# The last step of a triangular solve: the guess added by VectorE at the eviction, not by an identity product on TensorE

## The chip, the cores and the metric

The kernel runs on one core of a Trainium2 chip, as one program. Its engines are TensorE (PE in the profile, with its weight loads as PEld), VectorE (DVE), ScalarE (ACT), GpSimd (POOL) and SyncE (SP), which issues nearly all of the transfers. Each engine works through its own list of instructions in order and waits on semaphores. The metric is the device time of one execution in microseconds; less is better. Times of a run are compared with runs of the kernel before.

## The reference

The input is 4 sequences of 256 tokens with 256 features. A layer norm, then a gated delta rule with 16 key heads and 32 value heads of 128, then a layer norm and a mixture of experts. What matters here is the inner part, cut to this:

```python
T = solve_triangular(eye + M, eye, lower=True)      # M: strictly lower, from k k^T, decay, beta
v_c = einsum('bhnij,bhnjd->bhnid', T, v_beta)
k_cumdecay = einsum('bhnij,bhnjd->bhnid', T, k_beta * exp(g)[..., None])
def step(state, inp):
    attn = einsum('bhcd,bhed->bhce', q_i, k_i) * dec_i
    v_new = v_i - einsum('bhcd,bhde->bhce', kcd_i, state)
    out_i = einsum(q_i * exp(g_i), state) + einsum(attn, v_new)
    state = state * exp(g_last) + einsum(k_i * exp(g_last - g_i), v_new)
```

So for each chunk a triangular system is solved for `v_new`, and the output is made from it.

## The kernel before

The 256 tokens of a sequence are two chunks of 128 (c = 0 and 1). A **group** is one key head with its two value heads; there are 16 groups. In a group each of the 4 sequences b is a unit, and two units (b = 0, 1 or b = 2, 3) are a **pair**, handled by one set of instructions: 2 sequences times 2 value heads, 512 columns.

For a pair the inverse of the unit triangular matrix is built in f16 by seven rounds of doubling (steps `x`, `w` on PE; `xe` on ScalarE; `t`, `u` on VectorE). `u16` then holds the transposed inverse. The inverse is only good to f16, so each right-hand side is solved with one step of correction, per chunk c:

- `y0` (PE, L690): guess = inverse times right side, into the PSUM bank `Y_BANK`.
- `g` (ScalarE, L1029): copies it to the f16 tile `y0`.
- `y1` (PE, L702 and L705): applies the system to the guess in `R_BANK` (one identity product, eight products with `n16` and `nl16`), and at the end, L708, puts the guess itself into `Y_BANK` by a product with the identity.
- `rr` (VectorE, L1318): residual = values less `R_BANK`, f16.
- `y2` (PE, L714): adds inverse times residual to `Y_BANK`.
- `vn` (ScalarE, L1035): copies `Y_BANK` to the tile `vn`, which is `v_new`.

For c = 0 there follow `v0s` (GpSimd, L1617, `vn` times a decay), `p` (PE, L724, the state's part of the second right side) and `r1h` (VectorE, L1325), with which c = 1 begins. `o` (PE, L741 and L744) makes the output of a unit from `vn`, `v0s`, `at` and `qx`; `sqr`, `ln`, `rex` (ScalarE), `hsum` (GpSimd), `ss` (PE), `hz` and `ht` (VectorE) normalize and gate it; `hth` (ScalarE) and `htl` (GpSimd, L1565) split it in two f16 halves, and `proj` (PE, L767) projects it.

Beside this runs the input side of a later group: `fill` and `rest` (PE, L582) project a half kind of 512 tokens into one of two banks, `evict` (ScalarE, L919) takes it out with the last tap of a causal convolution of four taps, and three `tap` steps (VectorE, L1229) add the others from the same bank. There are 24 taps a group. The bank is free for the fill after the next when the third tap is done: fill number r waits until 3(r-2)+3 taps are done. Taps 2, 5, 8 and so on to 20 and 23 are thus the ones that PE waits for. `kk` (PE, L636 and L621), `mask` (VectorE, L1265), `cross` (ScalarE, L998) and `nt` (VectorE, L1274) prepare the triangular matrices of a unit.

The order is written out by hand: `TABLE` is one list of steps with their number, unit and lag in groups. `sequence()` walks the list 24 times, and each engine takes from it the steps that it has a function for, in that order. A step's place on its engine is therefore its place in the table, whichever engine that is. One walk is called a period below. The four `vn` steps of a walk are

```python
("tap", 0, None, 0), ("vn", 1, 2, 2), ("tap", 1, None, 0)
("t", 0, 2, 1), ("vn", 0, 0, 1), ("tap", 20, None, 0)
("y2", 1, 0, 1), ("eye", 1, 0, 0), ("t", 5, 2, 1), ... ("vn", 1, 0, 1)
("y2", 0, 2, 1), ("mask", 0, 0, 0), ("fill", 16, None, 0), ("vn", 0, 2, 1)
```

(chunk, first unit of the pair, lag). They are called C (1, 2, 2), A (0, 0, 1), B (1, 0, 1) and D (0, 2, 1) in the text. A step with lag L handles group n - L in walk n, so B, D and A occur in walks 1 to 16, C in walks 2 to 17, and the taps in walks 0 to 15.

Of the kernel before, what the change touches and what calls it, by code (L numbers as in the profile page):

```python
# [10 lines left out]
ALU = mybir.AluOpType  # L11
# [147 lines left out]
def build(nc, x, wqkvz, wba, convw, dtb, alog, normw, wout, wm, b1, b2, rw, rb, c32, eye16, lev, gsc, rowsc, out):  # L159
    ctx = ExitStack()  # L160
    with ctx:
# [75 lines left out]
        hz = sb("hz", [P, 2, 512])  # L237
# [165 lines left out]
        def turn(U):  # L403
            return unit_index(U) // 2 % 2
# [125 lines left out]
        def _(pe):  # L530
# [163 lines left out]
            def y1_(U, c):  # L694

                G, b = U
                wait_p(pe, s_y0, U, 2, c + 1)
                wait_u(pe, s_nl, (G, b + 1), 1, 1)
                if c == 0:
                    wait_p(pe, s_r, (G, b - 2), 2, 2)  # L700
                guess = y0[:].rearrange("p b v d -> p (b v d)")
                nc.tensor.matmul(R_BANK[:, :], eye[:, 0], guess, start=(c == 0), stop=False, skip_group_check=True)  # L702
                for n, (two, v) in enumerate(FOUR):
                    for part in (n16, nl16):
                        mm = nc.tensor.matmul(R_BANK[:, n * P:(n + 1) * P], part[:, turn(U), 4 * two + 2 * v + c], y0[:, two, v],  # L705
                                              start=False, stop=(part is nl16), skip_group_check=True)
                mm.then_inc(s_a, 1)
                nc.tensor.matmul(Y_BANK[:, :], eye[:, 0], guess, start=True, stop=False, skip_group_check=True)  # L708

            def y2_(U, c):  # L710

                wait_p(pe, s_r, U, 2, c + 1)
                for n, (two, v) in enumerate(FOUR):
                    mm = nc.tensor.matmul(Y_BANK[:, n * P:(n + 1) * P], u16[:, turn(U), 4 * two + 2 * v + c], rr[:, two, v],  # L714
                                          start=False, stop=True, skip_group_check=True)
                mm.then_inc(s_y, 1)

            def p(U, _):
# [137 lines left out]
        def _(act):  # L856
# [171 lines left out]
                    wait_p(act, s_a, U, 2, 1)  # L1028
                nc.scalar.copy(y0[:].rearrange("p b v d -> p (b v d)"), Y_BANK[:, :]).then_inc(s_y0, 1)  # L1029

            def solved(U, c):
                G, b = U
                wait_p(act, s_y, U, 4, 2 * c + 2)
                wait_u(act, s_o, (G, b - 3), 1, 1)
                nc.scalar.copy(vn[:, turn(U), :, :, c].rearrange("p b v d -> p (b v) d"),  # L1035
                               Y_BANK[:, :].rearrange("p (n d) -> p n d", n=4)).then_inc(s_vn, 1)

            def squares(U, _):
                G, b = U
                wait_u(act, s_o, U, 1, 1)  # L1040
# [58 lines left out]
            def end(F, i):  # L1099
                end_of(0, i)  # L1100

            attention({"gate": gate, "evict": evict, "hi": high_weights, "silu": silu, "nexp": norm, "cap": cap, "exb": row_factors,
                       "exp": factors, "cross": cross_, "n16": high_n, "xe": xe, "g": guess, "vn": solved,
                       "sqr": squares, "ln": log_mean, "rex": inverse_root, "hth": high_output, "end": end})

            def high(n):
# [20 lines left out]
        def _(dve):  # L1127
# [183 lines left out]
            def residual(U, c):  # L1311
# [4 lines left out]
                else:  # L1316
                    wait_p(dve, s_y, U, 4, 2)
                nc.vector.tensor_tensor(rr[:], values(U, c), R_BANK[:, :].rearrange("p (b v d) -> p b v d", b=2, v=2),  # L1318
                                        ALU.subtract).then_inc(s_r, 1)

            def right_side(U, _):
                G, b = U
                wait_p(dve, s_p, U, 1, 1)
                wait_p(dve, s_y, (G, b - 2), 4, 4)
                nc.vector.tensor_tensor(r1h[:], values(U, 1), R_BANK[:, :].rearrange("p (b v d) -> p b v d", b=2, v=2),  # L1325
                                        ALU.subtract).then_inc(s_r1h, 1)
# [153 lines left out]
            def end(F, i):  # L1480
                end_of(0, i)

            attention({"gate": gate, "tap": tap, "lo": low_weights, "sc": scalars, "nmul": norm, "mask": mask, "nt": decayed, "t": t,
                       "u": u, "rr": residual, "r1h": right_side, "hz": hz_, "ht": ht_,
                       "acc": acc_, "end": end})


# [239 lines left out]
```

## Time and profile before

| | |
|---|---|
| median of 3 runs | 1333.41 us (1332.9 to 1334.39) |
| the profiled execution: time, span | 1335.4 us, 1333.6 us |
| mean granted TensorE clock | 0.985 of full speed |
| busy share PE, PEld, DVE, ACT, POOL | 91%, 65%, 78%, 68%, 57% |
| chain that ended last, by engine | PE 73%, DVE 12%, issue 8%, ACT 3%, POOL 2% |
| one period in the middle of the run | 60.4 us |

The busy share is the time in which an engine had an instruction running. PE's is high for a reason beside work: matmuls overlap, and a row's duration holds time in which the next one already runs. Two starts in a row say more than one duration. The same holds for DVE and ACT, whose next instruction starts before the one ahead has ended. In the chain, "issue" is time in which an engine waited for nothing that the profile shows.

### The profile page before, as it was taken

The numbers are of one execution on the slowest core, as the hardware profiler recorded it, in microseconds if no ns is written. First come the engines' busy times: TensorE is split into PE (matmuls) and PEld (weight loads), VectorE is DVE, ScalarE is ACT, GpSimd is POOL, SyncE is SP. The second block draws the span as 40 slices with busy tenths as digits, with TensorE's granted clock in tenths as the row PEclk, the third lists the DMA queues.
The fourth block names the chain that finished last, engine by engine and source line by source line (L and its number), as shares of the span: only waits on it lengthen the run. The fifth ranks groups of instructions, "written<-read, shape, count | busy, mean of one in ns | idle before, by whom it ended". The sixth has DMA issues, their size and how long they took to land.

```text
span 1333.6 us, 32082 instructions
## 1 busy us (share of the span) xinstructions
PE 1217.2 (91%) x11612; PEld 863.4 (65%) x11612; DVE 1037.8 (78%) x1641; ACT 903.4 (68%) x1715; POOL 756.3 (57%) x792
## 2 busy tenths in 40 slices
PE   3678999999999999999999999999977589999997
PEld 2346676767767676767667676767665356666664
DVE  5586979888797979888897979798865676666565
ACT  2668888888978888888878888888863222222221
POOL 1255666667666766667665766666676667444100
PEclk9999999999999999999999999999999789999999
DMA  3111110101111111101110111100110056445331
GB/s 112 36 57 34 33 38 29 42 25 41 33 58 31 35 34 33 41 26 42 33 57 13 54 33 33 42 26 17 32 35 25 24 168 201 142 146 157 111 103 40
DMA packets 51623, 75.64 MB, mean 57 GB/s; under 512 B 8358, under 2 KB 27208, under 8 KB 51468
## 3 DMA queue, kind: packets, MB, share of 16 engines
q1 hardware_dynamic: 51396, 73.46, 18.0%
q8 instruction: 94, 1.54, 0.5%
q14 instruction: 61, 0.50, 0.1%
q10 hardware_dynamic: 72, 0.14, 0.0%
HBM read 72.26 MB, written 1.32 MB: 55 GB/s over the span
## 4 chain that ended last, share of the span: by engine, by line
PE 73%; DVE 12%; issue 8%; ACT 3%; POOL 2%; DMA 1%; SPq 1%; DVEq 0%; ACTq 0%; POOLq 0%
PE bank L582 15%; PE products L537 9%; PE bank L830 9%; DVE sil L1229 7%; PE products L767 6%; PE products L753 4%; PE products L741 4%; PE products L636 3%; PE bank L665 3%; PE bank L673 3%; PE bank L645 3%; PE bank L601 2%; PE bank L724 2%; PE products L621 2%; PE bank L705 2%
## 5 line engine op out<-in xcount | busy, mean ns | idle before, releaser
L582 PE MATMUL bank<-xT,whl 128*128 128x512 f16 x1152 | 296.6, 384 | 26.8 <-DVE sil L1229 26.7
L1229 DVE SCALAR_TENSOR_TENSOR sil<-bank,cw,sil 128x510 f32<-128x510 f32 (+2 forms) x384 | 283.4, 738 | 16.1 <-ACT sil L919 12.1
L582 PEld LDWEIGHTS bank<-xT,whl 128*128 128x128 f16 x1152 | 98.7, 98 | 125.3 <-DVE sil L1229 38.8
L1110 ACT ACTIVATE kq<-vtok 128x512 f16<-128x512 f32 x94 | 59.1, 630 | 177.1 <-DVE vtok L1499 176.0
L1288 DVE CAST_PREDICATED t<-levm,bank 128x512 f16<-128x512 uint8 x192 | 136.2, 710 | 39.0 <-PE bank L665 36.3
L1499 DVE SCALAR_TENSOR_TENSOR vtok<-products,b1s,zs 128x512 f32<-128x512 f32 x94 | 70.5, 750 | 87.4 <-PE products L537 87.1
L1300 DVE CAST_PREDICATED u<-levm,bank 128x512 f16<-128x512 uint8 x192 | 135.4, 705 | 0.0
L1017 ACT ACTIVATE x<-bank 128x512 f16<-128x512 f32 x160 | 96.2, 601 | 54.1 <-PE bank L645 52.7
L1565 POOL TENSOR_TENSOR hthl<-hz,hthl 128x512 f16<-128x512 f32 x64 | 74.2, 1159 | 93.8 <-ACT hthl L1054 93.8
L1624 POOL TENSOR_TENSOR at<-kqm,ex 128x256 f32<-128x256 f32 x128 | 102.7, 807 | 26.1 <-issue 14.5
L767 PE MATMUL products<-wohl,hthl 128*128 128x256 f16 x768 | 96.8, 277 | 9.3 <-POOL hthl L1565 8.9
L1588 POOL TENSOR_TENSOR hsq<-hsq,qsq 128x512 f32<-128x512 f32 x64 | 81.9, 1280 | 38.2 <-ACT hsq L1042 38.1
L919 ACT ACTIVATE sil<-bank,cw 128x512 f32<-128x512 f32 x128 | 87.7, 685 | 16.7 <-PE bank L582 15.8
L645 PEld LDWEIGHTS bank<-t,n 128*128 128x128 f16 x1536 | 67.6, 98 | 44.7 <-DVE t L1288 27.7
L1631 POOL TENSOR_TENSOR qx<-cross,exb 128x256 f32<-128x256 f32 x128 | 94.0, 734 | 2.3 <-ACT exb L985 2.3
L741 PE MATMUL products<-at,vn 128*128 128x128 f32 x512 | 82.4, 283 | 8.8 <-ACT cross L998 6.2
L977 ACT ACTIVATE ex<-grow,sc 128x128 f32<-128x128 f32 x256 | 86.3, 396 | 0.1
L645 PE MATMUL bank<-t,n 128*128 128x64 f16 x1536 | 77.3, 193 | 8.2 <-DVE t L1288 8.2
L767 PEld LDWEIGHTS products<-wohl,hthl 128*128 128x128 f16 x768 | 72.4, 99 | 19.0 <-issue 10.7
L1505 DVE SCALAR_TENSOR_TENSOR kq<-vtok,kq 128x512 f16<-128x512 f32 x94 | 80.3, 854 | 2.2 <-ACT kq L1110 2.1
L665 PEld LDWEIGHTS bank<-x,u 128*128 128x128 f16 x1280 | 53.5, 97 | 44.0 <-ACT x L1017 40.3
L741 PEld LDWEIGHTS products<-at,vn 128*128 128x128 f32 x512 | 67.1, 191 | 19.6 <-issue 11.3
(219 smaller groups left out, 3086.2 us busy)
## 6 DMA issues: line engine op xcount, KB each, us to landing
grow<-rowsc SPq DMA_DIRECT2D x64, 256.0 KB, 3.3
wt<-wqkvz SPq DMA_DIRECT2D x16, 768.0 KB, 4.4
wt<-wm SPq DMA_DIRECT2D x47, 256.0 KB, 2.8
zs<-gsc SPq DMA_DIRECT2D x35, 256.0 KB, 3.4
wo<-wout SPq DMA_DIRECT2D x16, 256.0 KB, 3.2
zs<-gsc SPq DMA_DIRECT2D x16, 224.0 KB, 3.1
zs<-gsc SPq DMA_DIRECT2D x16, 192.0 KB, 3.1
zs<-gsc SPq DMA_DIRECT2D x17, 160.0 KB, 3.3
```

The costliest lines, as they stand in the source:

```text
L537: mm = nc.tensor.matmul(dst, stationary(h, k), moving(l, k), start=(n == 0), stop=(n == len(terms) - 1))
L582: mm = nc.tensor.matmul(dst[:, :], whl[:, h, k, col:col + HD], xT[:, l, k, half * 512:(half + 1) * 512], start=(k == 0 and m == 0), stop=( ...
L645: mm = nc.tensor.matmul(X_BANK[:, m * 64:(m + 1) * 64], N[:, m], r, start=True, stop=True)
L741: mm = nc.tensor.matmul(dst, vn[:, turn(U), b % 2, v, c], at[:, nth(U), v, c], start=(v == 0 and c == 0), stop=(c == 0), skip_group_check= ...
L767: mm = nc.tensor.matmul(KB_BANK[:, c * D:(c + 1) * D], hthl[:, parity(U), h, v, c], wohl[:, q, l, v], start=(n == 0), stop=(n == len(terms ...
L830: mm = nc.tensor.matmul(bank[4 + t // 2][:, (t % 2) * D:(t % 2 + 1) * D], hid[:, n % HR, h, m * P:(m + 1) * P], lent[k % ring][:, l, D:2 * D],
L1017: ins = nc.scalar.mul(halves(X, n)[:, :, :, 0], packed(X_BANK, n), -1.0)
L1229: nc.vector.scalar_tensor_tensor(out=dst[:, :, late:S], in0=src[:, :, 0:S - late], scalar=cw[:, q, i, 3 - late:4 - late], in1=dst[:, :, la ...
L1288: nc.vector.copy_predicated(halves(t16[:, turn(U)], n)[:, :, :, 0], by4(2 * n, n), packed(X_BANK, n)).then_inc(s_tup, 1)
L1300: nc.vector.copy_predicated(halves(Ut, n)[:, :, :, 1], by4(2 * n + 1, n), packed(WT_BANK, n)).then_inc(s_uup, 1)
L1624: nc.gpsimd.tensor_tensor(at[:, nth(U), v], kqm[:, w, :, 1], ex[:, w, v], ALU.mult).then_inc(s_at, 1)
L1631: nc.gpsimd.tensor_tensor(qx[:, nth(U), v], cross[:, w], exb[:, w, v].unsqueeze(1).to_broadcast([P, 2, P]), ALU.mult).then_inc(s_qx, 1)
```

## The change

`y1` no longer puts the guess into `Y_BANK`; `y2` begins the sum in that bank itself; and `vn` moves from ScalarE to VectorE, where it adds the f16 tile `y0` to the bank as it evicts it. The table is not touched, so `vn` has the same place in it.

```diff
@@ in y1_ (PE)
                 mm.then_inc(s_a, 1)
-                nc.tensor.matmul(Y_BANK[:, :], eye[:, 0], guess, start=True, stop=False, skip_group_check=True)
@@ in y2_ (PE)
                     mm = nc.tensor.matmul(Y_BANK[:, n * P:(n + 1) * P], u16[:, turn(U), 4 * two + 2 * v + c], rr[:, two, v],
-                                          start=False, stop=True, skip_group_check=True)
+                                          start=True, stop=True)
@@ ScalarE
-            def solved(U, c):
-                G, b = U
-                wait_p(act, s_y, U, 4, 2 * c + 2)
-                wait_u(act, s_o, (G, b - 3), 1, 1)
-                nc.scalar.copy(vn[:, turn(U), :, :, c].rearrange("p b v d -> p (b v) d"),
-                               Y_BANK[:, :].rearrange("p (n d) -> p n d", n=4)).then_inc(s_vn, 1)
@@ VectorE
+            def solved(U, c):
+                G, b = U
+                wait_p(dve, s_y, U, 4, 2 * c + 2)
+                wait_u(dve, s_o, (G, b - 3), 1, 1)
+                nc.vector.tensor_tensor(vn[:, turn(U), :, :, c], Y_BANK[:, :].rearrange("p (b v d) -> p b v d", b=2, v=2), y0[:],
+                                        ALU.add).then_inc(s_vn, 1)
```

Each engine's list shows where the steps stand. The first place is VectorE at the end of the taps of a walk, around step A; `rr` is the residual of the same pair, `t` the first step of the next inverse, the `sil` rows are taps 18 to 21. Before:

```order
L1229 SCALAR_TENSOR_TENSOR sil<-bank,cw,sil 128x2x255
L1318 TENSOR_TENSOR rr<-vtok,bank 128x512
L1229 SCALAR_TENSOR_TENSOR sil<-bank,cw,sil 128x2x254
L1288 COPY_PREDICATED t<-levm,bank 128x512
L1229 SCALAR_TENSOR_TENSOR sil<-bank,cw,sil 128x2x253
L1300 COPY_PREDICATED u<-levm,bank 128x512
```

and of the change:

```order
L1221 SCALAR_TENSOR_TENSOR sil<-bank,cw,sil 128x2x255
L1310 TENSOR_TENSOR rr<-vtok,bank 128x512
L1221 SCALAR_TENSOR_TENSOR sil<-bank,cw,sil 128x2x254
L1280 COPY_PREDICATED t<-levm,bank 128x512
L1317 TENSOR_TENSOR vn<-bank,y 128x4x128
L1221 SCALAR_TENSOR_TENSOR sil<-bank,cw,sil 128x2x253
L1292 COPY_PREDICATED u<-levm,bank 128x512
```

The new `vn` stands ahead of tap 20, which frees a bank for PE.

The second place is VectorE at the beginning of the next group's taps, around step C. Before:

```order
L1274 TENSOR_TENSOR nt<-ex,kqm 128x512
L1229 SCALAR_TENSOR_TENSOR sil<-bank,cw,sil 128x2x255
L1229 SCALAR_TENSOR_TENSOR sil<-bank,cw,sil 128x2x254
L1288 COPY_PREDICATED t<-levm,bank 128x512
L1229 SCALAR_TENSOR_TENSOR sil<-bank,cw,sil 128x2x253
```

and of the change:

```order
L1266 TENSOR_TENSOR nt<-ex,kqm 128x512
L1221 SCALAR_TENSOR_TENSOR sil<-bank,cw,sil 128x2x255
L1317 TENSOR_TENSOR vn<-bank,y 128x4x128
L1221 SCALAR_TENSOR_TENSOR sil<-bank,cw,sil 128x2x254
L1280 COPY_PREDICATED t<-levm,bank 128x512
L1221 SCALAR_TENSOR_TENSOR sil<-bank,cw,sil 128x2x253
```

The `vn` of the pair before has come between tap 0 and tap 1, which work on the same rows of `sil`.

The third is VectorE around steps B and D; `u` 64x8x64 is the last round of an inverse, `kq` the normalized keys, `kqm` the step `mask`. Before:

```order
L1300 COPY_PREDICATED u<-levm,bank 128x16x32
L1303 CAST u<-bank 64x8x64
L1257 TENSOR_TENSOR kq<-sil,sq 128x4x256
L1348 SCALAR_TENSOR_TENSOR acc<-products,acc 128x512
L1318 TENSOR_TENSOR rr<-vtok,bank 128x512
L1265 TENSOR_TENSOR kqm<-products,cst 128x512
L1340 TENSOR_TENSOR hz<-hz,hsq 128x512
L1333 SCALAR_TENSOR_TENSOR hz<-products,zs 128x512
```

and of the change:

```order
L1292 COPY_PREDICATED u<-levm,bank 128x16x32
L1317 TENSOR_TENSOR vn<-bank,y 128x4x128
L1295 CAST u<-bank 64x8x64
L1249 TENSOR_TENSOR kq<-sil,sq 128x4x256
L1347 SCALAR_TENSOR_TENSOR acc<-products,acc 128x512
L1310 TENSOR_TENSOR rr<-vtok,bank 128x512
L1257 TENSOR_TENSOR kqm<-products,cst 128x512
L1317 TENSOR_TENSOR vn<-bank,y 128x4x128
L1339 TENSOR_TENSOR hz<-hz,hsq 128x512
L1332 SCALAR_TENSOR_TENSOR hz<-products,zs 128x512
```

B stands ahead of the last `u`, D between `mask` and `ht`.

## Rows read from the trace of the kernel before

**Rows 1.** The page: busy time of each engine over the span.

```profile
PE 1217.2 (91%) x11612; PEld 863.4 (65%) x11612; DVE 1037.8 (78%) x1641; ACT 903.4 (68%) x1715; POOL 756.3 (57%) x792
```

**Rows 2.** By stretch: us, busy us (count) PE, PEld, DVE, ACT, POOL; PEclk, DMA, GB/s.

```profile
402.49:462.87 60.38, 58.38 (x611) 42.43 (x611) 52.05 (x81) 51.66 (x100) 39.56 (x41) 1.00 0.12 37
402.50:411.00 8.50, 8.41 (x107) 5.40 (x108) 8.09 (x13) 7.71 (x18) 5.45 (x5) 1.00 0.01 2
433.40:462.87 29.47, 28.19 (x300) 19.51 (x299) 29.20 (x47) 24.37 (x48) 19.64 (x24) 1.00 0.14 40
```

**Rows 3.** Instructions of L708, L1035 and L1318: duration ns min/median/max, first and last start.

```profile
L708 PE MATMUL bank<-y,eye x64: 379/379/634, 96.3 to 1027.6; 128*128 128x512 f16 x64
...
L1035 ACT COPY vn<-bank x64: 573/585/588, 99.0 to 1028.9; 128x512 f32<-128x512 f32 x64
...
L1318 DVE TENSOR_TENSOR rr<-vtok,bank x64: 666/680/689, 97.8 to 1027.8; 128x512 f16<-128x512 f32 x64
```

**Rows 4.** Timeline around step A: start us, duration us, engine, line.

```profile
460.82 0.73 DVE L1229 SCALAR_TENSOR_TENSOR sil<-bank,cw,sil 128x508 f32<-128x508 f32 x1
460.98 0.38 PE L714 MATMUL bank<-rr,u 128*128 128x128 f16 x4
461.48 0.71 DVE L1288 CAST_PREDICATED t<-levm,bank 128x512 f16<-128x512 uint8 x1
462.09 0.72 DVE L1229 SCALAR_TENSOR_TENSOR sil<-bank,cw,sil 128x506 f32<-128x506 f32 x1
462.87 0.82 PE L582 MATMUL bank<-xT,whl 128*128 128x512 f16 x3 [0.21 <-DVE sil L1229]
```

**Rows 5.** Timeline around step C, VectorE and PE.

```profile
433.44 0.75 DVE L1229 SCALAR_TENSOR_TENSOR sil<-bank,cw,sil 128x510 f32<-128x510 f32 x1 [0.44 <-ACT sil L919]
434.31 0.75 DVE L1229 SCALAR_TENSOR_TENSOR sil<-bank,cw,sil 128x508 f32<-128x508 f32 x1
434.97 0.74 DVE L1288 CAST_PREDICATED t<-levm,bank 128x512 f16<-128x512 uint8 x1
435.59 0.74 DVE L1229 SCALAR_TENSOR_TENSOR sil<-bank,cw,sil 128x506 f32<-128x506 f32 x1
436.38 0.82 PE L582 MATMUL bank<-xT,whl 128*128 128x512 f16 x3
```

**Rows 6.** Timeline around step D.

```profile
422.50 0.69 DVE L1265 TENSOR_TENSOR kqm<-products,cst 128x512 f32<-128x512 f32 x1 [0.62 <-PE products L621]
423.11 0.68 DVE L1340 TENSOR_TENSOR hz<-hz,hsq 128x512 f32<-128x512 f32 x1
...
422.63 0.59 ACT L1035 COPY vn<-bank 128x512 f32<-128x512 f32 x1 [0.29 <-PE bank L714]
...
423.29 1.41 POOL L1617 TENSOR_TENSOR v0s<-vn,sc 128x512 f32<-128x512 f32 x1 [0.85 <-ACT vn L1035]
424.66 1.16 POOL L1565 TENSOR_TENSOR hthl<-hz,hthl 128x512 f16<-128x512 f32 x1
...
425.20 1.06 PE L724 MATMUL bank<-v0s,qx 128*128 128x128 f32 x8
426.09 1.47 PE L767 MATMUL products<-wohl,hthl 128*128 128x256 f16 x12
```

**Rows 7.** Timeline of PE: the removed product and what follows it, three places.

```profile
412.96 0.38 PE L708 MATMUL bank<-y,eye 128*128 128x512 f16 x1
413.18 0.40 PE L645 MATMUL bank<-t,n 128*128 128x64 f16 x8
...
420.69 0.38 PE L708 MATMUL bank<-y,eye 128*128 128x512 f16 x1
420.91 1.03 PE L636 MATMUL products<-kq 128*128 128x256 f32 x4
...
429.21 0.38 PE L708 MATMUL bank<-y,eye 128*128 128x512 f16 x1
429.58 1.10 PE L636 MATMUL products<-kq 128*128 128x256 f32 x4
```

More of the change, by code:

```diff
@@ L1102, in _ @@
             attention({"gate": gate, "evict": evict, "hi": high_weights, "silu": silu, "nexp": norm, "cap": cap, "exb": row_factors,
-                       "exp": factors, "cross": cross_, "n16": high_n, "xe": xe, "g": guess, "vn": solved,
+                       "exp": factors, "cross": cross_, "n16": high_n, "xe": xe, "g": guess,
                        "sqr": squares, "ln": log_mean, "rex": inverse_root, "hth": high_output, "end": end})
@@ L1483, in _ @@
             attention({"gate": gate, "tap": tap, "lo": low_weights, "sc": scalars, "nmul": norm, "mask": mask, "nt": decayed, "t": t,
-                       "u": u, "rr": residual, "r1h": right_side, "hz": hz_, "ht": ht_,
+                       "u": u, "rr": residual, "vn": solved, "r1h": right_side, "hz": hz_, "ht": ht_,
                        "acc": acc_, "end": end})
```

## The prediction

> **What bounds the kernel now.** I first read the busy times. PE is at 91% of the span, DVE at 78% [rows 1]. That alone would say that 64 matmuls less are a gain. PE's figure is inflated, though: a 512-column product is recorded with 379 ns [rows 3], yet the product after L708 starts 413.18 - 412.96 = 0.22 us after it, and 420.91 - 420.69 = 0.22 us at the second place [rows 7]. So one removed product is worth 0.22 us of PE at most, and all 64 of them 14.1 us.
>
> Next I asked for one period. The same fill starts at 402.49 and at 462.87, so a period lasts 60.38 us, in which DVE is busy 52.05 us [rows 2]: it has 8.3 us free, and four `vn` steps would want about 2.4. An average like this hides where the free time lies, so I cut the period. In the tap stretch, 433.40 to 462.87, DVE is busy 29.20 of 29.47 us [rows 2]: it has 0.27 us free in thirty. In the packed part, 402.50 to 411.00, PE is busy 8.41 of 8.50 us [rows 2]. The kernel thus has two regimes in each period: DVE paces the taps, PE what comes after. What the change is worth depends on which regime each of its pieces falls into.
>
> Then I read the places themselves, in the timeline. At the end of the taps PE starts a fill at 462.87, after 0.21 us idle put down to a tap; that tap started at 462.09 and lasted 0.72, so ended at 462.81 [rows 4]. At their beginning PE starts a fill at 436.38, and the tap that it needs ended at 435.59 + 0.74 = 436.33 [rows 5]. Both fills begin some 0.05 us after a tap's end: whatever delays those taps delays PE.
>
> **The price of the new step.** The trace has no sum of a PSUM bank and an f16 tile into an f32 tile. The nearest is `rr`, also a tensor-tensor operation of 512 columns with a PSUM bank and an SBUF tile, 680 ns [rows 3]. DVE starts the next instruction before the last has ended: 462.09 - 461.48 = 0.61 [rows 4], 435.59 - 434.97 = 0.62 [rows 5], 423.11 - 422.50 = 0.61 us [rows 6]. I take 0.60 as its turn on DVE and 0.68 until its result is there. Bounds: 0.60 if it overlaps as these do, 0.68 if its whole duration counts. On ScalarE the copy took 585 ns [rows 3].
>
> **The change part by part.**
>
> *Step A, ahead of tap 20.* The new `vn` goes between the `t` at 461.48 and the tap at 462.09. `y2` (L714) started at 460.98 with four products, 0.38 us in all, so its bank is complete at 461.36, 0.7 us before DVE comes to it [rows 4]: no wait, but the full 0.60 us, and the tap ends 0.60 us later. The fill moves from 462.87 to 463.47. After it PE is packed [rows 2] and cannot catch up. Behind `vn` on DVE wait tap 20, `u`, tap 21 and so on; all shift together. The walks with both step A and taps are 1 to 15: 15 x 0.60 = +9.0 us. PE's 0.22 us, saved here a little earlier, only makes it wait longer for the same tap: worth nothing.
>
> *Step C, between tap 0 and tap 1.* Tap 1 adds to what tap 0 has written, so it waits for its end: 433.44 + 0.75 = 434.19, started 434.31, while a tap's turn on DVE is only 434.97 - 434.31 = 0.66 us, so DVE was free at 434.10 [rows 5]. `vn` fits in part into this bubble: it starts at 434.10 and tap 1 at 434.70 in place of 434.31, that is +0.39 us. `t`, tap 2 and the fill at 436.38 shift with it. From there DVE has next to no free time until the end of the taps [rows 2], so the delay is still there at step A. Walks 2 to 15: 14 x 0.39 = +5.5 us. Bounds: 0.39 and 0.60 a walk (the bubble not used).
>
> *Step B* falls into the stretch where DVE waits for PE before the last round of `u`, and I cost it at nothing. The work that hides it is PE's way to that last round; without this cover it would cost its 0.60 us.
>
> *Step D.* DVE waits 0.62 us for PE [rows 6], does `mask` at 422.50, and now `vn` at 423.11 instead of ScalarE at 422.63 [rows 6]. Its result is there at 423.79, against 423.22 before: 0.57 us later. GpSimd waits for it: `v0s` started at 423.29, 0.07 after, and now starts at 423.86. With its 1.41 us it ends at 425.27, and `htl`, which started at 424.66, takes 1.16 us and now ends at 426.43. PE needs `htl` for `proj` at 426.09 [rows 6]: 0.35 us late (`p`, at 425.20, is late by 0.1 and hidden in it). `ht`, pushed to 423.71 by `vn`, ends at 424.39 and its halves are there before 425.27. If `v0s` takes less, D costs less: bounds 0 and 0.35. I take 0.35, since `v0s` lies beside the same DVE work as before. Walks 1 to 16: 16 x 0.35 = +5.6 us.
>
> *The product on PE.* The first two places, 412.96 and 420.69, lie after the packed part, with work right behind; I count 0.20 us each (bounds 0 and 0.22), since a copy on ScalarE and the keys' norm on DVE cap it a little. At the third, 429.21, the next product begins at 429.58, 0.37 us later and not 0.22 [rows 7]: it waits for something else, and the saving is lost. The fourth is at step A. Sum: 16 x 0.40 = -6.4 us.
>
> *The copy off ScalarE*: 64 x 0.585 us of an engine that is busy 68% [rows 1]. It stands on no path I could find, apart from making room at B, and I count nothing.
>
> Sum: 9.0 + 5.5 + 5.6 - 6.4 = +13.7 us. The profiled execution took 1335.4 us, so 1349.1; its time is 2.0 us above the median 1333.4, so I forecast **1347.1 us**, 1.0% slower.
>
> **A rule weighed against a row.** Two starts at 2.4 GHz (the granted clock is 1.00 in these stretches [rows 2]) lie 0.22 us apart for 512 columns [rows 7]. The Trainium skill, TensorE: Matmul & The Clock Gate, section Back-to-back issue gap, gives about 131 ns per matmul at N=512 in a sustained stream, and some 216 ns for an isolated one. By the first figure, as an estimate, the gain on PE would be 4.2 us and not 6.4, and the time 1349.3. The trace agrees with the second.
>
> **The rivals.**
>
> *PE is the bound and DVE has room.* The chain that ended last is 73% PE, and DVE has 8.3 us free in a period [rows 2]. If these took in all four `vn`, each product would give back its 0.22: 64 x 0.22 = -14.1 us, 1319.3. Against it stand the fills that start 0.05 us after a tap's end. It decides if taps 2 and 20 have at least 0.4 and 0.6 us of slack before their fills; a weaker form, in which only A, C and D are hidden and only two products count, gives -6.4 us, 1327.0. Chance together 0.08.
>
> *Little but A costs.* The shift at C is made up within the next 25 us, or D is absorbed: from 9.0 - 6.4 = +2.6 us to, with C kept in full, 9.0 + 5.5 - 6.4 = +8.1 us, 1336.0 to 1341.5. For it: DVE's 0.27 us free in the taps and `v0s` that may be shorter. Chance 0.20, of which 0.06 within 0.2% of before.
>
> *DVE is the bound throughout.* Every `vn` costs its turn and PE gives nothing back: 0.60 x (16 + 15 + 16 + 14) = +36.6 us, 1370.0. Against it: DVE waits 0.62 us for PE at D and 0.44 for ScalarE at C [rows 5, 6]. Some of it could still hold, if DVE comes to `vn` before `y2` is done and the taps stand behind it: at A there is 0.7 us to spare. A case of +20 us or more, 1353.4 and up, gets 0.10. DVE at 78% leads over PE's weight loads at 65% [rows 1]. The Trainium skill, Perfetto Trace Analysis, section Identifying the Most-Contended Engine, judges TensorE by its weight loads and would name DVE here, so it speaks against moving work there.
>
> **How the numbers follow.** The main case, DVE bound in the taps with step D late, has 0.62: its own bounds are 9.0 + 5.5 + 0 - 7.0 = +7.5 us, and with 0.68 a turn at A, 0.60 at C and one product of the two in vain, 10.2 + 8.4 + 5.6 - 3.2 = +21.0 us. The range for 8 in 10 leaves out the faster cases and the far end of the last rival: 1337 to 1354. A change of 0.2% (2.7 us) is about what a measurement of this kernel can tell from none. Faster 0.08, same 0.06, slower 0.86.
>
> **What the profile of the change should show.** A period of about 61.2 us in place of 60.38 (13.7 us over some 16 walks). L1317 on DVE 64 times with some 680 ns. At A the fill after tap 20 starts 0.6 us later against `t` of the same place, its wait grown from 0.21 to about 0.8. At C tap 1 starts 1.26 us after tap 0 in place of 0.87. At D `v0s` waits for DVE, and `proj` for `htl`. L708 gone, and at its third place the next product no earlier. The prediction is wrong if the fills behind taps 2 and 20 have come no later, if `vn` waits for `y2` on DVE, or if the shorter queue on ScalarE has brought evictions, and with them taps, forward.

## The result, and the profile after

| | before | after |
|---|---|---|
| median of 4 runs | 1333.9 us (1332.9 to 1338.49) | 1361.1 us (1357.56 to 1362.14) |
| the profiled execution: time, span | 1335.4 us, 1333.6 us | 1361.13 us, 1359.3 us |

The ratio is 1.0193, 95% interval 1.0173 to 1.0212. The change is slower, as forecast, but by 25.7 us of span in place of 13.7 us: 1361.1 us lies outside the range of 1337 to 1354.

The page of the changed kernel: busy times, the chain that ended last, and the row of the fills.

```profile
PE 1216.9 (90%) x11548; PEld 856.1 (63%) x11548; DVE 1079.5 (79%) x1705; ACT 874.6 (64%) x1651; POOL 757.6 (56%) x792
...
PE 65%; DVE 16%; issue 11%; ACT 4%; POOL 2%; DMA 1%; SPq 1%; DVEq 1%; ACTq 0%; POOLq 0%
...
L582 PE MATMUL bank<-xT,whl 128*128 128x512 f16 x1152 | 293.2, 380 | 39.8 <-DVE sil L1221 39.6
```

PE has 64 matmuls less than in [rows 1] and is busy for 0.3 us less, over a span that is 25.7 us longer; VectorE has 64 instructions and 41.7 us more. The fills, L582, idle 39.6 us for taps. On the page of before that figure is 26.7 us, and PE's share of the chain has gone down by 8 points from 73%.

The new `vn`, by its line: duration, what it waits for, who waits for it.

```profile
L1317 DVE TENSOR_TENSOR vn<-bank,y x64: 666/681/692, 97.6 to 1053.6; 128x512 f32<-128x512 f32 x64
its engine sat idle before it (us, times) until:
  PE bank L713: 0.5, 1
who waited for it (us, times):
  POOL v0s L1616: 87.0, 32
  PE products L740: 4.8, 15
```

It costs 681 ns, 1 ns from `rr` [rows 3], and never waits for `y2` save once. A step that never waits stands behind its data: it makes VectorE's own queue longer.

One period by stretch, from the fill behind tap 20 to the next (columns as in [rows 2]):

```profile
469.69:531.45 61.76, 58.53 (x606) 41.94 (x607) 54.27 (x85) 49.90 (x96) 39.72 (x41) 1.00 0.12 36
```

That is 1.38 us more than the 60.38 us of [rows 2], with VectorE 2.22 us busier: part of `vn` found room, most did not.

Step C, VectorE in the timeline, and PE's fill behind tap 2:

```profile
501.16 0.75 DVE L1221 SCALAR_TENSOR_TENSOR sil<-bank,cw,sil 128x510 f32<-128x510 f32 x1 [0.44 <-ACT sil L918]
501.82 0.68 DVE L1317 TENSOR_TENSOR vn<-bank,y 128x512 f32<-128x512 f32 x1
502.42 0.74 DVE L1221 SCALAR_TENSOR_TENSOR sil<-bank,cw,sil 128x508 f32<-128x508 f32 x1
503.07 0.72 DVE L1280 CAST_PREDICATED t<-levm,bank 128x512 f16<-128x512 uint8 x1
503.69 0.73 DVE L1221 SCALAR_TENSOR_TENSOR sil<-bank,cw,sil 128x506 f32<-128x506 f32 x1
...
504.48 0.82 PE L582 MATMUL bank<-xT,whl 128*128 128x512 f16 x3 [0.21 <-DVE sil L1221]
```

Tap 1 starts 502.42 - 501.16 = 1.26 us after tap 0, against 0.87 in [rows 5]. That is the +0.39 us forecast, and the fill still begins 0.06 us after tap 2 has ended.

Step A:

```profile
529.47 0.71 DVE L1280 CAST_PREDICATED t<-levm,bank 128x512 f16<-128x512 uint8 x1
530.08 0.67 DVE L1317 TENSOR_TENSOR vn<-bank,y 128x512 f32<-128x512 f32 x1
530.67 0.72 DVE L1221 SCALAR_TENSOR_TENSOR sil<-bank,cw,sil 128x506 f32<-128x506 f32 x1
531.45 0.82 PE L582 MATMUL bank<-xT,whl 128*128 128x512 f16 x3 [0.81 <-DVE sil L1221]
```

From `t` to the fill it is 1.98 us, against 1.39 in [rows 4]: +0.59. The idle time before the fill has grown from 0.21 to 0.81 us.

Step D:

```profile
489.64 0.69 DVE L1257 TENSOR_TENSOR kqm<-products,cst 128x512 f32<-128x512 f32 x1 [0.56 <-PE products L621]
490.25 0.68 DVE L1317 TENSOR_TENSOR vn<-bank,y 128x512 f32<-128x512 f32 x1
490.85 0.68 DVE L1339 TENSOR_TENSOR hz<-hz,hsq 128x512 f32<-128x512 f32 x1
...
491.01 1.43 POOL L1616 TENSOR_TENSOR v0s<-vn,sc 128x512 f32<-128x512 f32 x1 [1.37 <-DVE vn L1317]
...
492.40 1.16 POOL L1564 TENSOR_TENSOR hthl<-hz,hthl 128x512 f16<-128x512 f32 x1
492.54 1.13 PE L723 MATMUL bank<-v0s,qx 128*128 128x128 f32 x8
...
493.81 1.36 PE L766 MATMUL products<-wohl,hthl 128*128 128x256 f16 x11
```

From `kqm` to `proj` (L766) it is 4.17 us. In [rows 6] it was 3.59: 0.58 us, not 0.35.

**The ledger.** The other VectorE instructions have the same order in both kernels, so the trace of after can be laid over that of before, instruction by instruction, and the lateness (start after less start before) read off at each step. What a regular walk (walk 6) adds, and the totals:

```
                              predicted   read
at A (tap 20)                   +0.60    +0.60
B to mask (products saved)      -0.40    -0.05
at D (mask to the next tap 0)   +0.35    +0.58   (0.31 + 0.27)
at C (tap 1)                    +0.39    +0.40
one walk                        +0.94    +1.53

late at tap 0 of walk 2                    -1.4 us
late at tap 0 of walk 15                  +20.4 us   (21.8 in 13 walks, 1.85 of it in one stretch of walk 12)
late at the last u of walk 15             +21.2 us   (961.64 of before)
the stretch behind it                      +4.6 us   (961.64 to the vtok at 1124.81 of before)
late from there to the end                +25.7 us
```

So the walks from 2 to 14 make 1.5 us each, walk 12 loses 1.85 us more, and the last stretch adds 4.6 us.

### The profile page after: what moved, and what is told of

The parts are those of the page before. It is cut to its first block, busy times and chain, and to the rows that moved or that the text cites. A ratio compares the mean times of both kernels' runs of the same rounds, so it can differ in the third digit from the quotient of the medians.

```text
span 1359.3 us, 31954 instructions
## 1 busy us (share of the span) xinstructions
PE 1216.9 (90%) x11548; PEld 856.1 (63%) x11548; DVE 1079.5 (79%) x1705; ACT 874.6 (64%) x1651; POOL 757.6 (56%) x792
## 4 chain that ended last, share of the span: by engine, by line
PE 65%; DVE 16%; issue 11%; ACT 4%; POOL 2%; DMA 1%; SPq 1%; DVEq 1%; ACTq 0%; POOLq 0%
PE bank L582 13%; DVE sil L1221 9%; PE products L537 8%; PE bank L829 8%; PE products L766 6%; PE products L752 4%; PE products L636 4%; PE bank L665 3%; PE bank L673 3%; PE products L740 3%; PE bank L645 2%; PE bank L723 2%; PE bank L601 2%; PE products L621 2%; DVE vn L1317 2%
## 5 line engine op out<-in xcount | busy, mean ns | idle before, releaser
L582 PE MATMUL bank<-xT,whl 128*128 128x512 f16 x1152 | 293.2, 380 | 39.8 <-DVE sil L1221 39.6
L582 PEld LDWEIGHTS bank<-xT,whl 128*128 128x128 f16 x1152 | 97.3, 98 | 134.5 <-DVE sil L1221 52.8
L766 PE MATMUL products<-wohl,hthl 128*128 128x256 f16 x768 | 96.5, 276 | 12.1 <-POOL hthl L1564 9.8
L645 PEld LDWEIGHTS bank<-t,n 128*128 128x128 f16 x1536 | 65.6, 98 | 47.3 <-DVE t L1280 34.4
L1616 POOL TENSOR_TENSOR v0s<-vn,sc 128x512 f32<-128x512 f32 x32 | 39.2, 1226 | 87.0 <-DVE vn L1317 87.0
L766 PEld LDWEIGHTS products<-wohl,hthl 128*128 128x128 f16 x768 | 71.9, 99 | 23.9 <-issue 15.6
L645 PE MATMUL bank<-t,n 128*128 128x64 f16 x1536 | 78.0, 194 | 8.2 <-DVE t L1280 8.2
L665 PEld LDWEIGHTS bank<-x,u 128*128 128x128 f16 x1280 | 54.1, 98 | 46.0 <-ACT x L1016 34.9
```

The costliest lines, as they stand in the source:

```text
L582: mm = nc.tensor.matmul(dst[:, :], whl[:, h, k, col:col + HD], xT[:, l, k, half * 512:(half + 1) * 512], start=(k == 0 and m == 0), stop=( ...
L645: mm = nc.tensor.matmul(X_BANK[:, m * 64:(m + 1) * 64], N[:, m], r, start=True, stop=True)
L665: mm = nc.tensor.matmul(X_BANK[:, m * 64:(m + 1) * 64], Ut[:, m], halves(X, n)[:, m, :, 0], start=True, stop=True)
L766: mm = nc.tensor.matmul(KB_BANK[:, c * D:(c + 1) * D], hthl[:, parity(U), h, v, c], wohl[:, q, l, v], start=(n == 0), stop=(n == len(terms ...
```

## The experiments

Twelve kernels were run; the last of them, e_last_old, is the change itself once more, since its edit has no effect (see below). "Late per walk" is read as above, over the regular walks.

| label | median us (runs) | before us | ratio, 95% interval |
|---|---|---|---|
| e_only_a | 1344.0 (6) | 1335.38 | 1.0069, 1.0052 to 1.0086 |
| e_only_b | 1334.99 (12) | 1335.38 | 0.9999, 0.9984 to 1.0013 |
| e_only_c | 1340.63 (9) | 1335.38 | 1.0040, 1.0024 to 1.0055 |
| e_only_d | 1344.99 (6) | 1335.38 | 1.0068, 1.0046 to 1.0089 |
| e_product_out | 1334.69 (12) | 1335.31 | 0.9997, 0.9984 to 1.0010 |
| e_copy_moved | 1362.0 (4) | 1335.31 | 1.0195, 1.0176 to 1.0214 |
| e_c_ahead | 1336.0 (12) | 1337.79 | 0.9990, 0.9980 to 1.0000 |
| e_d_behind | 1345.79 (6) | 1337.79 | 1.0062, 1.0044 to 1.0080 |
| e_a_behind | 1343.83 (6) | 1337.79 | 1.0048, 1.0034 to 1.0062 |
| e_short_hi | 1335.9 (12) | 1337.79 | 0.9993, 0.9982 to 1.0004 |
| e_short_hi_product_out | 1333.01 (12) | 1336.81 | 0.9974, 0.9962 to 0.9986 |
| e_last_old | 1361.47 (5) | 1336.43 | 1.0192, 1.0171 to 1.0212 |

**One place at a time.** The whole change (product left out, sum made on VectorE) is made for one of the four steps; the other three keep the product and ScalarE's copy.

```diff
+ON_DVE = ((0, 0),)                  # A; B ((1, 0),), C ((1, 2),), D ((0, 2),)
@@ y1_
+                if (c, b) not in ON_DVE:
                     nc.tensor.matmul(Y_BANK[:, :], eye[:, 0], guess, start=True, stop=False, skip_group_check=True)
@@ y2_
-                                          start=False, stop=True, skip_group_check=True)
+                                          start=(c, U[1]) in ON_DVE, stop=True, skip_group_check=True)
```

> The change at step A alone (15 walks with taps): VectorE adds the guess there, the product of that pair is out; B, C and D stay as before. In the trace of the whole change the walks gained 0.60 us between tap 18 and the start of u at this place. Theory P (each place has its own price, prices add): +9 us, 15 x 0.60. Rival R (VectorE is short of time as a whole, so that one step of four is mostly taken in by its 8 us free in a period, and the fourth is what breaks it): +0 to +3 us.

> The change at step B alone. Theory P: VectorE waits for PE there anyway, so the new step is free; the product saved on PE is lost at the next wait for an eviction on ScalarE (the step x). 0 us, within 1 of before. If the products are worth their 0.22 us on PE: -3.5 us (16 x 0.22). Rival R as for A: 0 to +3.

> The change at step C alone (14 walks with taps). The whole change showed +0.39 us between tap 0 and tap 2. Theory P: +5.5 us, 14 x 0.39, less whatever ScalarE gains in walk 16. Rival R: 0 to +1.

> The change at step D alone. The whole change showed proj 0.57 us late here against the products ahead of it. Theory P: the result of the new step is there 0.57 us later, v0s and htl on GpSimd pass all of it on, because proj waited for htl in the kernel before already (0.28 us from the end of the GpSimd row, the same as the shortest such gap); one product saved gives 0.06 to 0.2 back. 16 x 0.45 = +7 us, bounds 5.6 and 9. If my first estimate of 0.35 us and 0.2 back were right: +2.4 us.

A alone is late by 0.60 us a walk, C by 0.39 to 0.40, D by 0.57 less 0.06, and B is free. The ratios' excesses add up: 0.69 + 0 + 0.40 + 0.68 = 1.77%, against 1.93% for all four, which is within their intervals. Each place has its own price, and apart from walk 12 (below) the prices add. D is nearly as dear as A, where the prediction had it at little more than half. In time D took 9.6 us, above its bounds of 5.6 and 9; 3.0 us of it arise in the last stretch (below).

**The product and the copy apart.** In the first kernel only L708 goes, and `y2` begins the bank itself; ScalarE copies as before. The output lacks the guess, so only the correction is passed on. In the second the product stays, and VectorE copies the bank instead of ScalarE.

```diff
@@ e_product_out: y1_, y2_
-                nc.tensor.matmul(Y_BANK[:, :], eye[:, 0], guess, start=True, stop=False, skip_group_check=True)
...
-                                          start=False, stop=True, skip_group_check=True)
+                                          start=True, stop=True)
@@ e_copy_moved: solved, on VectorE
+                nc.vector.tensor_copy(vn[:, turn(U), :, :, c].rearrange("p b v d -> p (b v) d"),
+                                      Y_BANK[:, :].rearrange("p (n d) -> p n d", n=4)).then_inc(s_vn, 1)
```

> The kernel before without the identity product L708 at all four places, vn still copied by ScalarE: it leaves the guess out of the sum. Theory P (the saving is lost at the next wait: x on ScalarE at B, the keys' norm at D, the log of the mean at C, tap 20 at A): -1 us, between 0 and -2. My prediction counted 0.20 us at two places: -6.4 us. PE as the bound throughout: -14 us.

> The product L708 kept, only the eviction vn moved to VectorE as a plain copy (nothing is left out, the sum is made on PE). Theory P: VectorE's turn alone makes the loss, so it is about as slow as the change, +24 to +28 us. If the sum of two operands is what costs on VectorE (a longer turn than a copy's), clearly less: under +15.

The 64 products are worth nothing that can be measured: 0.9997, and 0.06 us in a regular walk. Moving the copy alone costs all that the change costs, 1.0195 against 1.0193. In its time the change is therefore a step moved to VectorE and nothing else; the addition that it does there costs nothing measurable, and the products that it saves gave nothing measurable either.

**Why the saved products give nothing.** The first place was followed along PE in before. This is what stands behind L708 there (its own row and the next are in [rows 7]):

```profile
413.13 0.40 ACT L937 CAST v<-bank 128x256 f16<-128x256 f32 x1
413.18 0.40 PE L645 MATMUL bank<-t,n 128*128 128x64 f16 x8
413.38 0.64 ACT L938 COPY vtok<-bank 128x512 f32<-128x512 f32 x1
413.86 0.66 ACT L1017 ACTIVATE x<-bank 128x512 f16<-128x512 f32 x1
414.58 0.40 PE L665 MATMUL bank<-x,u 128*128 128x64 f16 x8
```

L645 ended at 413.58, but ScalarE took its bank out only at 413.86, right behind other copies, and PE's L665 needs that `x`. ScalarE has a full queue there, so L645 may come 0.2 us earlier to no avail. If this is the cause, less work on ScalarE ahead of it must bring the saving back. So one ScalarE step ahead of that place, the conversion of the high half `whl` of the next group's weights, was made short. It is made in two pieces (k = 0 and 1) of 768 columns; the short kernel leaves out 760 columns of the first piece, from the second group on. The second kernel of the pair leaves out the products as well, and with them the guess.

```diff
-                    nc.scalar.mul(whl[:, 0, k], wt[:, k], SPLIT).then_inc(s_hi, 1)
+                    short = F != (None, 0) and k == 0
+                    dst, src = (whl[:, 0, k, 0:8], wt[:, k, 0:8]) if short else (whl[:, 0, k], wt[:, k])
+                    nc.scalar.mul(dst, src, SPLIT).then_inc(s_hi, 1)
```

> The base of a pair: the kernel before, in which the first of the two high halves of the next weights (hi, k = 0) converts 8 columns instead of 768, from the second group on; it leaves out most of that half of the conversion. It frees ScalarE for some 0.5 us a walk just ahead of the step x, for which PE waits behind the first saved product. By itself 0 to -3 us.

> The other half of the pair: the short hi, and without the product L708 at all four places (it leaves out the guess in the sum and most of one high half of the weights). Theory P (the saving of the first product is lost only because PE waits behind it for ScalarE, which is full there): 0.16 to 0.35 us a walk less than the short hi alone, -2.5 to -5.5 us against it. Rival (the product's time is not worth anything on PE, overlap or else): the same as the short hi alone, as the products out made no difference to the kernel before.

The same place in e_short_hi:

```profile
411.73 0.64 ACT L938 COPY vtok<-bank 128x512 f32<-128x512 f32 x1
411.94 0.38 PE L708 MATMUL bank<-y,eye 128*128 128x512 f16 x1
412.16 0.40 PE L645 MATMUL bank<-t,n 128*128 128x64 f16 x8
412.39 1.11 PE L601 MATMUL bank<-sq,cst 128*128 128x256 f32 x4
412.59 0.60 ACT L1019 ACTIVATE x<-bank 128x512 f16<-128x512 f32 x1 [0.23 <-PE bank L645]
```

Now `x` waits for PE (0.23 us idle), and in the walks from 2 to 14 the kernel without the products gains some 0.20 us between the taps' end and `mask` against the one with them. Of it 0.12 to 0.15 us are gained at the first place, by the last `u`; without the short conversion nothing is gained there (within 0.02 us). The other 0.06 us are gained at the second place, with the short conversion as without it. So at the first place ScalarE's queue took the saving, and a shorter one gives back 0.14 of the 0.22 us. That is shown. The medians, 1333.01 against 1335.9 us, also point this way, but part of those 2.9 us arises in the first walks and in the last stretch: at tap 0 of walk 15 the two differ by 2.5 us, and other places of a walk gave some of the 0.20 back.

At the second place the rows of e_product_out name the cap:

```profile
417.66 1.40 DVE L1256 TENSOR_TENSOR kq<-sil,sq 128x1024 f32<-128x1024 f32 x1 [0.85 <-ACT sq L965]
419.12 1.13 PE L636 MATMUL products<-kq 128*128 128x256 f32 x4
```

L708 is gone, and L636 starts 0.06 us after the end of `kq` (419.06), the keys' norm on VectorE that it reads. No run made `kq` earlier, so this place is read from rows and not tested.

**Three other orders.** Each moves one step in the table.

```diff
@@ e_c_ahead (C alone on VectorE)
-    ("tap", 0, None, 0), ("vn", 1, 2, 2), ("w", 0, 0, 1), ("tap", 1, None, 0),
+    ("vn", 1, 2, 2), ("tap", 0, None, 0), ("w", 0, 0, 1), ("tap", 1, None, 0),
@@ e_d_behind (D alone)
-    ("fill", 16, None, 0), ("vn", 0, 2, 1), ("end", 30, None, 1), ("fill", 17, None, 0), ("ht", 0, 3, 2),
+    ("fill", 16, None, 0), ("end", 30, None, 1), ("fill", 17, None, 0), ("ht", 0, 3, 2), ("vn", 0, 2, 1),
@@ e_a_behind (A alone)
-    ("vn", 0, 0, 1), ("tap", 20, None, 0), ("x", 1, 2, 1),
+    ("tap", 20, None, 0), ("x", 1, 2, 1), ("vn", 0, 0, 1),
```

> Step C alone on VectorE as in the run with C alone (+5.3 us), but its place in the table is ahead of tap 0 and not behind it. VectorE waits there 0.44 us for ScalarE's eviction, and y2 has been done for 2 us. Theory P (the price is the turn of 0.60 us less the idle time that the place has): VectorE is free at 432.31 + 0.60 = 432.91, the step is over at 433.51, tap 0 started at 433.44: 14 x 0.07 = +1 us. Rival R (any step more on VectorE costs its share): +5 us as before.

> Step D alone on VectorE, but behind ht instead of ahead of it. Theory P (D costs by the lateness of vn, which v0s and htl on GpSimd pass on to proj): vn is there another 0.60 us later, v0s perhaps shorter than 1.41 us; 0.85 to 1.15 us a walk, +13 to +18 us. Rival (D costs because it pushes ht and with it the high half of the output back by a turn): ht is at its old place again, so the loss is gone, 0 to +2 us.

> Step A alone on VectorE, but behind tap 20 instead of ahead of it, so that the bank is freed at its old time. If A costs only because tap 20 is late: near 0. Theory P: u, which the next w on PE waits for, is 0.60 us late instead, and v0s comes 0.65 us later, with p behind it: 0.45 to 0.65 us a walk, +7 to +10 us, about as with A ahead of the tap (+9.2).

C ahead of tap 0 fills VectorE's wait for ScalarE's eviction (0.44 us in [rows 5]): 0.07 us late per walk instead of 0.40, and 0.9990 in time. The trace of e_c_ahead puts both taps into one row without a wait:

```profile
433.78 1.60 DVE L1233 SCALAR_TENSOR_TENSOR sil<-bank,cw,sil 128x510 f32<-128x510 f32 x2
435.30 0.72 DVE L1292 CAST_PREDICATED t<-levm,bank 128x512 f16<-128x512 uint8 x1
```

A is as dear behind tap 20 as ahead of it, about 0.60 us a walk (the intervals of 1.0048 and 1.0069 overlap). The taps behind it are packed, so moving the step past one bank release did not hide it. In time it is 6.0 us, just under the 7 to 10 expected. Whether the next bank release or the later `u` passes the 0.60 us on was not separated.

D behind `ht` is late by 0.74 us a walk, 0.23 us more than ahead of it (0.57 - 0.06). That is more, as theory P says, but less than its 0.85 to 1.15; in time it is 8.0 us against the 13 to 18 expected. Its rows, from e_d_behind:

```profile
424.68 0.68 DVE L1353 TENSOR_TENSOR hz<-hz,hsq 128x512 f32<-128x512 f32 x1
425.28 0.69 DVE L1331 TENSOR_TENSOR vn<-bank,y 128x512 f32<-128x512 f32 x1
...
426.05 1.05 POOL L1630 TENSOR_TENSOR v0s<-vn,sc 128x512 f32<-128x512 f32 x1 [1.97 <-DVE vn L1331]
...
427.05 1.17 POOL L1578 TENSOR_TENSOR hthl<-hz,hthl 128x512 f16<-128x512 f32 x1
...
428.48 0.93 PE L769 MATMUL products<-wohl,hthl 128*128 128x256 f16 x7 [0.15 <-issue]
```

`ht` and its half on ScalarE are back at their old place here, and `proj` is later all the same: what sets D is when `vn` releases `v0s`. `v0s` takes only 1.05 us here, with no `ht` beside it, and that takes back 0.36 of the 0.60 us of one more turn on VectorE.

**The last stretch.** The stretch that adds 4.6 us was first put down to the last group's own `vn` steps, since PE has little to do there and a chain of single steps sets the time. The last kernel was to make the change in groups 0 to 14 and keep the product and ScalarE's copy in group 15.

```diff
+LAST = 15
@@ y1_
+                if U[0] == LAST:
                     nc.tensor.matmul(Y_BANK[:, :], eye[:, 0], guess, start=True, stop=False, skip_group_check=True)
@@ y2_
+                                          start=U[0] != LAST, stop=True, skip_group_check=True)
```

> Groups 0 to 14 as in the change; the last group, 15, keeps the product L708 and ScalarE's copy, so walk 16 and the work after the taps run on the old steps. In the profile of the change the last group's stretch adds 5.0 us (the shift against before grows from 20.6 us after the last tap walk but one to 25.6 at the end), where one regular walk adds 1.5. Theory L (the last group is a chain of single steps, in which each vn of 680 ns that starts after VectorE's turn, in place of 585 ns at once on ScalarE, is late for what follows): most of it goes, 3 to 4 us, with 1.5 left that walk 15's taps add as any walk: 1357 to 1358.5 where the change takes 1361.1, ratio to before 1.0165 to 1.018. Rival (the last stretch is later for another reason, such as TensorE's lower clock there, and stays): 1360 to 1361.5.

The edit does nothing. A group is the pair `(None, g)` in this program, so `U[0]` is never equal to `LAST`. The trace of e_last_old has the same counts of instructions as the change, with all 64 `vn` on VectorE, those of the last group too:

```profile
PE 1220.5 (90%) x11548; PEld 857.3 (63%) x11548; DVE 1079.2 (79%) x1705; ACT 873.2 (64%) x1651; POOL 756.0 (56%) x792
...
L1331 DVE TENSOR_TENSOR vn<-bank,y x64: 666/681/691, 98.8 to 1053.9; 128x512 f32<-128x512 f32 x64
```

So theory L and its rival were not tested. What the run does show is that the change repeats: 1361.47 us against 1361.1, again 1.9 us lost in walk 12, and 4.4 us in the last stretch against 4.6. The windows of the first part of this stretch, up to the experts' start, in before, in the change and in e_last_old (columns as in [rows 2]):

```profile
961.97:1062.20 100.23, 70.63 (x738) 56.75 (x736) 61.14 (x105) 49.11 (x97) 68.71 (x74) 0.91 0.11 30
```

```profile
983.05:1086.45 103.40, 71.84 (x731) 58.54 (x729) 64.83 (x111) 45.81 (x91) 69.07 (x74) 0.89 0.10 29
```

```profile
983.96:1087.11 103.15, 72.12 (x729) 58.44 (x730) 64.64 (x111) 45.38 (x90) 68.89 (x75) 0.88 0.09 29
```

How late each kernel was at the last `u` of walk 15 (961.64 of before), and what the whole stretch from there to the `vtok` at 1124.81 adds against the 163.2 us that it lasts in before, in all the profiles, one execution each. Part 1 ends at the VectorE step at 1062.11 of before; the last column is the mean granted clock in part 1.

```
kernel                   late at its start   stretch   part 1   part 2   clock in part 1
before                         0.0              0         0        0         0.915
e_short_hi_product_out        -3.2            +0.8      +1.7     -0.9        0.900
e_product_out                 -2.3            +2.0      +1.7     +0.3        0.879
e_short_hi                    -0.8            +1.2      +2.2     -1.0        0.901
e_c_ahead                     +0.6            +1.1      -0.1     +1.2        0.915
e_only_b                      +0.9            -0.1      +1.7     -1.9        0.883
e_only_c                      +3.8            -1.4       0.0     -1.4        0.915
e_only_d                      +7.4            +3.0      +2.9     +0.1        0.884
e_a_behind                    +7.4            +2.4      +2.1     +0.2        0.879
e_d_behind                    +8.1            +4.5      +3.2     +1.3        0.901
e_only_a                      +9.5            -2.6      +0.1     -2.7        0.915
the change                   +21.2            +4.6      +3.1     +1.5        0.886
e_last_old (the change)      +21.7            +4.4      +3.0     +1.4        0.885
e_copy_moved                 +22.2            +5.1      +3.9     +1.2        0.886
```

Three things can be read from it.

- First, 1.0 us of the 4.6 is the price of D in walks 15 and 16: at these two places all four kernels with D on VectorE at its place in the table (the change twice, e_copy_moved, e_only_d) lose 0.5 or 0.6 and then 0.4 us, and a kernel with D on ScalarE loses nothing.
- Second, part 1 goes with the granted clock. The four kernels with a mean of 0.915 there, e_only_a and e_only_c among them, are within 0.1 us of before; the ten profiles with 0.879 to 0.901 take 1.7 to 3.9 us more, the three whose `vn` are all on ScalarE (e_product_out, e_short_hi and e_short_hi_product_out) among them. Beside D's 1.0 us the change loses some 2.1 us in this part, as these do. No run held the clock, so that it is the cause is argued and not shown.
- Third, part 2 lies behind the last `vn` and still moves by -2.7 to +1.5 us, and there the clock does not rank the kernels; what decides it stays open.

In the first column the four single places were late by 9.5 + 0.9 + 3.8 + 7.4 = 21.6 us when the stretch began, and the whole change by 21.2.

**No version beats the kernel before.** B alone and C ahead of tap 0 lie within 0.2% of it.

## Why the prediction was wrong

**Right.** The reading of the regimes held. VectorE paces the taps, and both fills stayed 0.06 us behind a tap's end. Steps A and C cost 0.60 and 0.40 us a walk, where 0.60 and 0.39 were forecast (e_only_a, e_only_c). B is free (e_only_b). The turn of 0.60 and the result after 0.68 us were right (681 ns), as was the third place of the product, where the next one comes no earlier. The most-contended rule of the Trainium skill (Perfetto Trace Analysis, section Identifying the Most-Contended Engine) pointed the right way too, and so the trace agrees with it in sign. It ranks whole engines and tells no places apart, and B cost nothing while A cost its full turn.

**The term for the products, -6.4 us.** The step that failed: "I count 0.20 us each (bounds 0 and 0.22), since a copy on ScalarE and the keys' norm on DVE cap it a little". They cap it nearly altogether: all the products together give 0.06 us a walk, under 1 us in all (e_product_out), and the pair of e_short_hi shows that ScalarE's queue takes it at the first place. The lower bound, 0, was the value to take. PE was packed by its rows, but a packed PE behind which stands an engine that is itself packed gives nothing back: 8.41 of 8.50 us busy [rows 2] said that PE had work, not that its work set the end. The same rows have ScalarE at 7.71 and VectorE at 8.09 of 8.50. Over the regular walks 2 to 14 this is 4.5 us of the miss (13 x 0.35).

**The term for D, 0.35 us.** The step that failed: "`htl` ... takes 1.16 us and now ends at 426.43. PE needs `htl` for `proj` at 426.09 [rows 6]: 0.35 us late". It set a row's end against another row's start. In [rows 6] `htl` ends at 425.82 and `proj` starts at 426.09, and I took these 0.27 us for slack. In the change `htl` ends at 493.56 and `proj` starts at 493.81, again 0.25 us after it. In neither trace does any of the 64 `proj` start less than 0.25 us after its `htl` has ended, not even where PE stood idle for it, so at most 0.02 or 0.03 us of the 0.27 was slack: `proj` had been waiting for `htl` all along, and the whole 0.57 us by which `vn` comes later passes to it. The Trainium skill, Perfetto Trace Analysis, section Per-instruction lifecycle, says that the time in which a semaphore's update spreads lies outside the profiled window. The trace agrees that there is time between two such rows, but it is not one figure for two engines: `ss` on PE starts 0.05 us after its `hsum` on GpSimd has ended at the shortest, and `p` 0.10 us after `v0s`. D measures 0.57 us a walk before the saving (e_only_d). Over walks 2 to 14 that is 3.0 us more than counted (13 x 0.23). The count of 16 walks was off by one too: in walk 1 there is no `ht` of an earlier group behind D, and e_only_d loses nothing there.

**Not in the sum.** Walk 12 lost 1.85 us to a collision of VectorE and GpSimd (below). The stretch behind the last `u` of walk 15 added 4.6 us where the sum had 0.1; 1.0 of it is D again, some 2 us go with a lower granted clock, and the rest stays open. The parts make 4.5 + 3.0 + 1.85 + 4.5 = 13.9 us, and the miss is 12.0. The difference lies in the first two walks, which the sum had 0.55 us late and which end 1.4 us early: A costs its 0.59 us in walk 1 as in every other, but between tap 0 and tap 19 of that walk the change gained 1.6 us. e_product_out and e_a_behind gain 1.7 us there too, e_only_a 0.2; no run shows why. That the miss is not 14 us is thus luck of the start.

**The rivals.** "PE is the bound and DVE has room" and "Little but A costs" fell, since C and D cost in full. "DVE is the bound throughout" was nearest in time, and the measured time lies in its case of 1353.4 us and up, which had 0.10; yet it is there for another reason than the rival gave: B is free, and D's price runs through GpSimd and not through taps. The rival had the clause that counted, that PE gives nothing back.

## What to carry to other kernels

Before a saving on a busy engine is put into a sum, follow it to the next wait that ends on another engine, and ask whether that engine could have come earlier; if it is packed too, the saving is worth nothing. Slack between a producer's end and a consumer's start has to be measured against the shortest such gap of the same two instructions anywhere in the trace, for that much of it is no slack. Another pair on the same two engines won't do: GpSimd to PE has 0.05 us for one pair and 0.25 for another. And an experiment's time says something only if its trace shows the edit: the counts of instructions show that e_last_old is the change unaltered. A step moved to an engine costs one turn in each place where that engine paces others and nothing where it waits, so it should be placed into the waits first: C ahead of tap 0 costs 0.07 us, behind it 0.40.

## What the runs showed of the hardware

The keys' `kq` on VectorE and GpSimd's `qsq`, both tensor-tensor operations on SBUF, hold each other up, and who starts first wins. In walk 0, where they lie 7 us apart, `kq` takes 1.23 us and `qsq` 1.90. In all later walks but one `kq` begins 0.3 to 0.4 us before `qsq`, as here in the change:

```profile
860.31 1.43 DVE L1249 TENSOR_TENSOR kq<-sil,sq 128x1024 f32<-128x1024 f32 x1 [0.83 <-ACT sq L965]
860.62 2.88 POOL L1579 TENSOR_TENSOR qsq<-kq 128x1024 f32<-128x1024 f32 x1
```

In walk 12 of the change `qsq` began 0.04 us ahead:

```profile
796.78 1.90 POOL L1579 TENSOR_TENSOR qsq<-kq 128x1024 f32<-128x1024 f32 x1
796.82 2.93 DVE L1249 TENSOR_TENSOR kq<-sil,sq 128x1024 f32<-128x1024 f32 x1 [1.18 <-ACT sq L965]
```

The second of the two takes 1.0 to 1.5 us more than the first: `qsq` 2.88 against 1.90, `kq` 2.93 against 1.43. PE waits for `kq` and for nobody's `qsq` just then, so the same collision costs nothing in one order and 1.5 us in the other. It is no chance event: the order turns over in walk 12 in all three traces with the four steps moved (the change, its repeat e_last_old, and e_copy_moved), and in none of the others. The Trainium skill, SBUF — State Buffer, section SBUF: two separate sides, says that the port pair shared by the two engines is an exclusive lock, which the first to start holds for its whole instruction; the rows agree, in either order. `v0s` shows it on a smaller scale: 1.41 to 1.43 us beside `ht`, 1.05 without. An instruction's duration in the trace is that of its neighbourhood: in walk 12 `kq` was 0.34 us later than the taps ahead of it, which turned the order over and cost another 1.5 us.
